# Attention scores as fp32 products of two tokens, values streamed against loaded probabilities, context divided on VectorE as it leaves PSUM

## Chip, cores and metric

One NeuronCore of one Trainium2 chip. The metric is the device time of one execution in microseconds (us); each kernel is given by the median of several runs.

## What is computed

A transformer block on x of shape (4, 512, 512), that is 2048 tokens of 512 features, in fp32. The attention is not over the sequence: each token has 32 heads of 16 features, and the 32 heads of a token attend to each other.

```python
q = (x @ wq.T + bq).reshape(B, S, 32, 16)      # k and v the same way
scores = einsum('bshd,bstd->bsht', q, k) / 4   # 32 x 32 for each token
context = einsum('bsht,bstd->bshd', softmax(scores), v).reshape(B, S, 512)
x = layernorm(x + context)
h = silu(x @ dq(w1).T) * (x @ dq(w2).T)        # 1376 hidden
x = layernorm(x + h @ dq(w3).T)
```

dq quantises blocks of 64 weights to the 16 NF4 levels and back, in the kernel. The layernorm has no gain and no offset.

## The kernel before

The order on each engine is written out by hand, with semaphores. There are three stages.

**Projection.** 48 turns tau: 4 blocks of 512 tokens, in each 4 turns for q, 4 for k, 4 for v. `project(tau)` makes 12 fp32r products of 512 columns into one of three PSUM banks. For q and k, three bf16 parts are split off: `part_high` (ScalarE, L810), `part_rest` (VectorE, L1186), `part_middle` (ScalarE, L819), `part_low` (VectorE, L1194); SyncE stores them to `qk_parts` in DRAM in runs of 272 bf16 (L588). ScalarE's `value` (L824) gives v, stored to `v_blocks`.

**NF4 levels.** 19 units of weights have 15 levels each, 285 in all. ScalarE's `steep` (L769) makes `nf_y`, VectorE's `lift` (L1154) takes it into `nf_acc`; three `nf_y` buffers stand between them. The tables LV_P, LV_A, LV_T and LV_F say how many levels are done in each turn of the projection, of the attention, at its end and in each step of the feed-forward: 59, 55, 5 and 166. GpSimd normalises a unit ahead of its levels and scales it after them.

**Attention.** 32 groups G of 64 tokens (16 token indices i in each of four quarters q). `load_stacks` (L423) brings, for every half block (4 groups), 12 pieces from `qk_parts` into `q_st` and `k_st`: 128 partitions hold the six products of bf16 parts, so one bf16 product of 128 rows gives the scores of one token. `scores(G)` (L1019) makes 64 products with 32 stationary and 32 streaming columns, four quarters in the four column groups of the array. VectorE: `highest`, `shift`, and a group later, after ScalarE's `exp`, `swap`, which transposes blocks of 32x32 to `probT`. `values(G)` (L1034) makes 16 fp32 products: stationary is `v_bd`, 128 rows (4 quarters of 32 heads) by 68 columns (4 times 16 features and a column of ones, for the sum), streaming is `probT` of 32 columns. ScalarE's `context` (L837) copies the 68x512 result to `ctx`. Once per block, `turn(("ct", b, k))` transposes heads back in five turns of 7, 7, 7, 7 and 4 heads, and VectorE's `add_context` (L1218) takes the reciprocal of the sums, multiplies and adds to the residual `part`. Then come the moments (VectorE), the norm (ScalarE) and `turn(("xt", ...))`, which transposes x1 for the feed-forward.

PE's order in a group is scores(G), ct turns, values(G - 2), xt turns. `v_bd_0` lies over memory that the projection uses, so GpSimd's `clear` (L716) and the load of it come after the last projection turns; the second `v_bd` after all parts and values are stored. `q_st`, `k_st` of the first half block are loaded from tau 37 on (FIRST_LOAD).

**Feed-forward.** 44 steps, each of 24 products for gate and up and 12 for down, with 512 columns, while the levels that are left go on. The last block's context turns and x1 turns lie in steps 2 to 7.

Of the kernel before, what the change touches and what calls it, by code (L numbers as in the profile page):

```python
# [14 lines left out]
P = 128  # L15
# [19 lines left out]
def layer_kernel(nc, x, wq, bq, wk, bk, wv, bv, w1, w2, w3, out):  # L35
# [18 lines left out]
    MV = Q4 * DV  # L54

    Q_TERMS = (0, 1, 2, 0, 1, 0)
    K_TERMS = (0, 0, 0, 1, 1, 2)  # L60

    TS = TB + 16
# [32 lines left out]

    def turns_of(u):

        kind, g, _ = UNITS[u]
        return [("f", u, s) for s in range(2 if kind == "w" else -(-len(GROUPS[g]) // 2))]
# [14 lines left out]
    def parts_of(u):  # L114
# [6 lines left out]
    NQK, NV, NPV = 5, 4, 4  # L121
# [5 lines left out]
    qk_d = nc.dram_tensor("qk_parts", [2, NHB, 3 * E, TS], BF16, kind="Internal").ap()  # L127
# [35 lines left out]
    HEADS = [range(0, 7), range(7, 14), range(14, 21), range(21, 28), range(28, 32)]  # L163
    CT_AT, XT_AT, MOMENTS_AT, NORM_AT, F_AT = {}, {}, {}, {}, {}
    for b in range(NBK - 1):
        for k in range(len(HEADS)):
            CT_AT.setdefault(8 * b + 10 + k // 2, []).append(("ct", b, k))
        MOMENTS_AT[8 * b + 12] = b
        NORM_AT[8 * b + 13] = b
        for c in range(KC):  # L170
            XT_AT.setdefault(8 * b + 14 + c // 2, []).append(("xt", b, c))

    LATE = {8 * b + 8 + k: 8 * b + 13 for b in range(NBK - 1) for k in range(2)}
    CONTEXT_AT = {}
# [59 lines left out]
    with ExitStack() as both, ExitStack() as proj, ExitStack() as att:  # L234
# [19 lines left out]
        crec = sb("crec", [P, 2, 7 * Q4], F32)  # L254
# [12 lines left out]
        room = sb("room", [P, 2 * H * (TS - TB) // 2 + MV * TI], F32, proj)  # L267
# [3 lines left out]
        qk_p = sb("qk_p", [P, NQK, 3, BK + TS - TB], BF16, proj)  # L271
        qk_r = sb("qk_r", [P, 3, BK], F32, proj)
# [40 lines left out]
        s_zero = sem("s_zero")  # L313
# [1050 lines left out]
```

## Time and profile before

| | |
|---|---|
| median of 3 runs | 787.52 us (786.13 to 788.67) |
| the profiled execution: its own time | 788.01 us |
| its span (first to last instruction) | 786.2 us |
| PE busy, share of the span | 732.7 us, 93% |
| VectorE (DVE) | 633.4 us, 81% |
| ScalarE (ACT) | 484.6 us, 62% |
| GpSimd (POOL) | 106.8 us, 14% |
| mean granted TensorE clock | 0.862 of full |
| DMA | 117.89 MB in 89474 packets |

In the span the projection ends at 165.6 us, the attention runs to 380 us, the feed-forward to the end. A busy PE is one with instructions in flight, not one at its peak. A time in the rows is counted from the span's start.

### The profile page before, as it was taken

Reading aid. Unit: us, or ns where it says so; the run is one execution under the profiler, and the core shown is the slowest. Engines: PE = TensorE matmul, PEld = TensorE weight load, DVE = VectorE, ACT = ScalarE, POOL = GpSimd, SP = SyncE. Lnnn points to the kernel's source line nnn. Section 1 sums busy time; section 2 is a strip of 40 time slices with the busy share of each in tenths; the row PEclk is TensorE's granted clock in tenths of the full one; section 3 lists DMA queues with packets and bytes.
Section 4 is the critical chain, followed back from the end, with each engine's and each line's share of the span. In section 5 each row is a group of like instructions: output and inputs, shape, how many; then the busy total and the mean of one; then the engine's idle time right before and its main releaser. Section 6 shows DMA issues by size and latency. Waiting matters only on the chain.

```text
span 786.2 us, 14305 instructions
## 1 busy us (share of the span) xinstructions
PE 732.7 (93%) x5688; PEld 625.5 (80%) x5688; DVE 633.4 (81%) x876; ACT 484.6 (62%) x650; POOL 106.8 (14%) x101
## 2 busy tenths in 40 slices
PE   4899999966999989999999999999999999999983
PEld 4778788856999989999888877887887788888761
DVE  2699999975888988988888899999977986554386
ACT  3588979773645636546853878877756775333134
POOL 2011012113101101111101121121201111000022
PEclk9999999995555655555799999999999999999995
DMA  9964455999797695995413371211514010330347
GB/s 219 223 182 146 134 166 167 250 305 271 166 261 189 184 283 134 269 216 202 163 26 122 120 230 54 81 39 31 173 59 155 1 61 21 134 119 13 121 147 160
DMA packets 89474, 117.89 MB, mean 150 GB/s; under 512 B 24768, under 2 KB 70848, under 8 KB 86496
## 3 DMA queue, kind: packets, MB, share of 16 engines
q1 hardware_dynamic: 88272, 114.88, 51.6%
q10 hardware_dynamic: 1136, 2.10, 1.2%
q8 instruction: 45, 0.74, 0.4%
q14 instruction: 21, 0.17, 0.1%
HBM read 76.42 MB, written 38.86 MB: 147 GB/s over the span
## 4 chain that ended last, share of the span: by engine, by line
PE 54%; DVE 18%; issue 11%; ACT 8%; DMA 4%; SPq 4%; POOL 1%; DVEq 0%; POOLq 0%; ACTq 0%
PE ps_p L1043 10%; DVE nf_acc L1166 8%; PE ps_s L947 7%; PE ps_s L945 7%; PE ps_s L946 7%; PE ps_p L945 5%; PE ps_p L947 5%; PE ps_p L946 5%; ACT nf_y L777 4%; PE ps_s L1030 3%; PE ps_t L968 2%; DMA qk_parts<-qk_p 2%; DVE part L1298 2%; DMA k_st<-qk_parts 1%; ACT part L852 1%
## 5 line engine op out<-in xcount | busy, mean ns | idle before, releaser
L1166 DVE SCALAR_TENSOR_TENSOR nf_acc<-nf_y,nf_acc 128x1024 f32<-128x1024 f32 (+4 forms) x266 | 298.5, 1122 | 37.6 <-ACT nf_y L777 28.3
L777 ACT ACTIVATE nf_y<-nf_w,bound_b 128x1024 f32<-128x1024 f32 (+4 forms) x285 | 288.9, 1047 | 9.7 <-DVE nf_acc L1162 3.4
L1043 PE MATMUL ps_p<-probT,v_bd 128*68 128x32 f32 x1024 | 125.7, 301 | 7.9 <-issue 7.9
L1043 PEld LDWEIGHTS ps_p<-probT,v_bd 128*68 128x68 f32 x1024 | 122.7, 211 | 9.4 <-issue 8.0
L945 PE MATMUL ps_p<-x_hl,w_hl 128*128 128x512 f32 x192 | 77.6, 404 | 6.1 <-DVE w_hl L1184 4.1
L695 POOL TENSOR_TENSOR nf_w<-nf_w,nf_rec 128x1024 f32<-128x1024 f32 (+4 forms) x19 | 39.5, 2080 | 320.1 <-DVE nf_rec L1150 320.1
L1325 DVE TENSOR_TENSOR silu<-silu,ps_s 128x512 f32<-128x512 f32 (+1 forms) x44 | 30.1, 684 | 61.5 <-PE ps_s L947 61.5
L927 ACT ACTIVATE hid_hl<-silu 128x512 fp32r<-128x512 f32 (+1 forms) x44 | 27.8, 632 | 77.6 <-DVE silu L1325 77.6
L947 PE MATMUL ps_p<-x_hl,w_hl 128*128 128x512 f32 x192 | 75.5, 393 | 0.0
L945 PE MATMUL ps_s<-x_hl,f_ha 128*128 128x512 f32 x192 | 75.4, 393 | 0.0
L946 PE MATMUL ps_p<-x_hl,w_hl 128*128 128x512 f32 x192 | 75.3, 392 | 0.0
L947 PE MATMUL ps_s<-x_hl,f_la 128*128 128x512 f32 x192 | 75.1, 391 | 0.0
L946 PE MATMUL ps_s<-x_hl,f_ha 128*128 128x512 f32 x192 | 75.0, 391 | 0.0
L834 ACT ACTIVATE prob<-prob 128x512 f32<-128x512 f32 x32 | 20.4, 638 | 86.4 <-DVE prob L1209 86.4
L922 ACT ACTIVATE silu<-ps_s 128x512 f32<-128x512 f32 (+1 forms) x44 | 26.2, 595 | 66.1 <-PE ps_s L947 66.0
L702 POOL TENSOR_TENSOR nf_acc<-nf_acc,nf_max 128x1024 f32<-128x1024 f32 (+4 forms) x19 | 37.6, 1977 | 209.7 <-DVE nf_acc L1166 209.6
L947 PE MATMUL ps_s<-x_hl,f_lb 128*128 128x512 f32 (+1 forms) x160 | 62.4, 390 | 0.0
L945 PE MATMUL ps_s<-x_hl,f_hb 128*128 128x512 f32 (+1 forms) x160 | 62.4, 390 | 0.0
L946 PE MATMUL ps_s<-x_hl,f_hb 128*128 128x512 f32 (+1 forms) x160 | 62.3, 390 | 0.0
L1030 PE MATMUL ps_s<-k_st,q_st 128*32 128x32 bf16 x2048 | 44.5, 249 | 9.0 <-issue 6.9
L1030 PEld LDWEIGHTS ps_s<-k_st,q_st 128*32 128x32 bf16 x2048 | 40.0, 171 | 13.5 <-issue 11.5
L945 PEld LDWEIGHTS ps_p<-x_hl,w_hl 128*128 128x128 f32 x192 | 36.5, 190 | 14.7 <-issue 5.4
(110 smaller groups left out, 1253.1 us busy)
## 6 DMA issues: line engine op xcount, KB each, us to landing
x_hl<-x_parts SPq DMA_DIRECT2D x10, 2048.0 KB, 8.5
qk_parts<-qk_p SPq DMA_DIRECT2D x64, 204.0 KB, 2.6
q_st<-qk_parts SPq DMA_DIRECT2D x48, 272.0 KB, 6.8
k_st<-qk_parts SPq DMA_DIRECT2D x48, 272.0 KB, 7.2
x_parts<-x_st SPq DMA_DIRECT2D x16, 512.0 KB, 4.4
nf_w<-in_L_ffn_w SPq DMA_DIRECT2D x24, 256.0 KB, 3.0
dequantised<-nf_acc SPq DMA_DIRECT2D x10, 512.0 KB, 2.6
v_blocks<-v_t SPq DMA_DIRECT2D x16, 256.0 KB, 3.5
```

The lines of the kernel that those rows point to most:

```text
L695: pool.tensor_tensor(v, v, nf_rec[0:p, 0:w // QBLOCK].unsqueeze(2).to_broadcast([p, w // QBLOCK, QBLOCK]), ALU.mult).then_inc(s_nnorm, 1)
L702: pool.tensor_tensor(acc, acc, nf_max[0:p, u % 2, 0:w // QBLOCK].unsqueeze(2).to_broadcast([p, w // QBLOCK, QBLOCK]), ALU.mult).then_inc(s ...
L777: act.activation(nf_y[0:p, at % NY, 0:w], nf_w[0:p, u % 2, 0:w], ACT.Identity, bias=bound_b[0:p, i:i + 1], scale=STEEP).then_inc(s_ny, 1)
L922: act.activation(silu[0:rows, s % 2], ps_s[0:rows, 0], ACT.Silu).then_inc(s_silu, 1)
L927: act.activation(hid_hl[0:rows, s % 2, 0], silu[0:rows, s % 2], ACT.Copy).then_inc(s_hh, 1)
L945: pe.matmul(dst, wh, rh, start=start, stop=False)
L946: pe.matmul(dst, wh, rl, start=False, stop=False)
L947: return pe.matmul(dst, wl, rh, start=False, stop=stop)
L1030: t = pe.matmul(ps_s[32 * q:32 * q + 32, G % 2, i * H:(i + 1) * H], q_st[:, :, s], k_st[:, :, s], start=True, stop=True)
L1043: t = pe.matmul(ps_p[0:MV, (G + 3) % NPV, i * H:(i + 1) * H], v_bd[hb % 2][:, :, g * GI + i], probT[:, G % 2, i], start=True, stop=True)
L1166: dve.scalar_tensor_tensor(out=acc, in0=y, scalar=float(NF4[i + 1]), in1=acc, op0=ALU.min, op1=ALU.max).then_inc(s_nacc, 1)
L1325: dve.tensor_tensor(h, h, ps_s[0:rows, 1], ALU.mult).then_inc(s_hid, 1)
```

## The change

- q and k stay fp32. ScalarE alone evacuates them (`queries_keys`, one operation), VectorE evacuates v (`value` moves from ScalarE). Each of the 32 q and k tiles is stored by one DMA of 128x16 runs of 36 fp32 (144 bytes; 32 tokens and 4 of padding) instead of two of 128x3 runs of 544 bytes.
- Scores: a product covers two tokens j. Stationary is `q_st`, 32 rows (2 tokens of 16 features) by 32 heads; streaming is `k_st`, 32 rows by 64 columns, zero where row and column are of different tokens. The four quarters sit on the diagonal of the array (rows 32q, columns 32q). 32 products per group instead of 64, fp32 instead of bf16.
- Values: `probT` (32 columns) is stationary and `v_bd` (68 columns, 68 fp32 apart) streams; four tokens go to the four column groups. VectorE's new `divide(G)` takes reciprocals of the 128x16 sums and multiplies 128x256 out of PSUM into `ctmp`. PE's new `back(G)` makes 4 transposes of `ctmp` (64 stationary, 128 streaming columns), and `context` copies 64x512.
- The context turns are four of eight heads, and `add_context` is one addition.
- Loads: queries one DMA per half block, keys eight of 16 partitions, zeros of `k_st` by GpSimd. The first keys, values and queries are loaded from tau 29, 31, 33, 37, 39 on, and `v_bd_0` is cleared at tau 12.
- Levels: LV_P 72, LV_A 45, LV_T 5, LV_F 163 of its 166.

```diff
-    TS = TB + 16
+    MC = Q4 * D
+    VS = TI + 4
+    J2, TN = 2, TI // 2
+    KS = TN + 4
...
+    FIRST_LOADS = {3 * KC * (NBK - 1) + at: what for at, what in ((-7, "keys 0"), (-5, "values 0"), (-3, "keys 1"),
+                                                                  (1, "queries 0"), (3, "queries 1"))}
-    LV_P = [1, 1, 1, 1, 1, 1, 1, 1, 2, 2, 2, 2] * NBK
+    LV_P = [0, 0, 0, 1, 2, 2, 2, 1, 2, 2, 2, 2] + [2, 2, 1, 2, 2, 1, 2, 2, 1, 2, 1, 2] * (NBK - 1)
     LV_P[-3:] = [1, 0, 0]
-    LV_A = [2] * GG
+    LV_A = [2, 1] * (GG // 2)
...
@@ sync
-                    for e in range(2):
-                        sp.dma_start(qk_d[i, 2 * b + e].rearrange("(a f) t -> f a t", a=3)[P * m:P * m + P],
-                                     qk_p[:, n % NQK, :, TB * e:TB * e + TS]).then_inc(s_stq[n % NQK], 16)
+                    sp.dma_start(qk_d[i, 2 * b:2 * b + 2, :, :, Q4 * m:Q4 * m + Q4].rearrange(
+                        "e q j r h n -> (r h) (e q j) n"), qk_p[:, n % NQK]).then_inc(s_stq[n % NQK], 16)
...
@@ scalar
+                act.activation(qk_p[:, n % NQK, :, 0:TN], ps_p[:, tau % 3].rearrange("p (a n) -> p a n", n=TN),
+                               ACT.Identity, bias=bias[:, i, m:m + 1]).then_inc(s_qh, 1)
...
@@ tensor
-                for i in range(GI):
+                for i in range(GI // J2):
                     for q in range(Q4):
-                        s = q * TI + g * GI + i
-                        t = pe.matmul(ps_s[32 * q:32 * q + 32, G % 2, i * H:(i + 1) * H],
-                                      q_st[:, :, s], k_st[:, :, s], start=True, stop=True)
+                        rows, n = slice(32 * q, 32 * q + 32), GI // J2 * g + i
+                        t = pe.matmul(ps_s[32 * q:32 * q + 32, G % 2, J2 * H * i:J2 * H * (i + 1)],
+                                      q_st[hb % 2][rows, :, n],
+                                      k_st[hb % 2][rows, :, :, n].rearrange("d j h -> d (j h)"), start=True, stop=True)
...
@@ tensor
-                wait(pe, s_ctx, G - NPV + 1)
+                wait(pe, s_evac, G - 1)
                 for i in range(GI):
-                    t = pe.matmul(ps_p[0:MV, (G + 3) % NPV, i * H:(i + 1) * H], v_bd[hb % 2][:, :, g * GI + i],
-                                  probT[:, G % 2, i], start=True, stop=True)
+                    a, j = divmod(i, 4)
+                    token = TN * (i % J2) + GI // J2 * g + i // J2
+                    t = pe.matmul(ps_p[32 * j:32 * j + 32, G % 2, a * MV:(a + 1) * MV], probT[:, G % 2, i],
+                                  v_bd[hb % 2][:, :, token], start=True, stop=True)
                 t.then_inc(s_pv, 1)
+            def back(G):
+                pe.wait_ge(s_evac, G + 1)
+                wait(pe, s_ctx, G - 1)
+                for a in range(4):
+                    t = pe.transpose(ps_p[0:MC, 2 + G % 2, P * a:P * a + P], ctmp[:, G % NCT, a * MC:(a + 1) * MC],
+                                     ident[:])
+                t.then_inc(s_back, 1)
...
@@ vector
+            def divide(G):
+                dve.wait_ge(s_pv, G + 1)
+                src = ps_p[:, G % 2, 0:4 * MV].rearrange("p (a q d) -> p a q d", q=Q4, d=DV)
+                rec = crec[:, G % 2].rearrange("p (a q) -> p a q", q=Q4)
+                dve.reciprocal(rec, src[:, :, :, D]).then_inc(s_crec, 1)
+                dve.wait_ge(s_crec, G + 1)
+                wait(dve, s_back, G - NCT + 1)
+                dve.tensor_tensor(ctmp[:, G % NCT].rearrange("p (a q d) -> p a q d", q=Q4, d=D), src[:, :, :, 0:D],
+                                  rec.unsqueeze(3).to_broadcast([P, 4, Q4, D]), ALU.mult).then_inc(s_evac, 1)
```

PE's order from the end of the projection into the attention, of the kernel before (the last number of a row is the count of the same instruction in a row; `ps_s` are scores, `ps_p` the values' result):

```order
601 L1030 MATMUL ps_s<-k_st,q_st 32x32 x192
602 L1043 MATMUL ps_p<-probT,v_bd 68x32 x16
603 L1030 MATMUL ps_s<-k_st,q_st 32x32 x64
604 L1043 MATMUL ps_p<-probT,v_bd 68x32 x16
605 L1030 MATMUL ps_s<-k_st,q_st 32x32 x64
```

The same place in the changed kernel:

```order
601 L1012 MATMUL ps_s<-k_st,q_st 32x64 x96
602 L1029 MATMUL ps_p<-v_bd,probT 32x68 x16
603 L1012 MATMUL ps_s<-k_st,q_st 32x64 x32
604 L1029 MATMUL ps_p<-v_bd,probT 32x68 x16
605 L1038 MATMUL ps_p<-ident,ctmp 64x128 x4
```

A group is 32 products of 64 columns and 16 of 68 instead of 64 of 32 and 16 of 32, and four transposes are added one group later.

VectorE's order in the attention before, two groups with context turns:

```order
197 L1205 TENSOR_REDUCE smax<-ps_s 128x16
198 L1215 STREAM_TRANSPOSE probT<-prob 128x512
199 L1209 TENSOR_TENSOR prob<-ps_s,smax 128x512
200 L1225 RECIPROCAL crec<-ps_t 128x28
201 L1228 TENSOR_TENSOR y_tmp<-ps_t,crec 128x448
202 L1232 TENSOR_TENSOR part<-part,y_tmp 128x7x4x16
203 L1225 RECIPROCAL crec<-ps_t 128x28
204 L1228 TENSOR_TENSOR y_tmp<-ps_t,crec 128x448
205 L1232 TENSOR_TENSOR part<-part,y_tmp 128x7x4x16
206 L1166 SCALAR_TENSOR_TENSOR nf_acc<-nf_y,nf_acc 128x1088
```

And a plain group and one with context turns in the changed kernel:

```order
154 L1200 TENSOR_REDUCE smax<-ps_s 128x16
155 L1210 STREAM_TRANSPOSE probT<-prob 128x512
156 L1204 TENSOR_TENSOR prob<-ps_s,smax 128x512
157 L1167 SCALAR_TENSOR_TENSOR nf_acc<-nf_y,nf_acc 128x1088 x2
158 L1218 RECIPROCAL crec<-ps_p 128x16
159 L1221 TENSOR_TENSOR ctmp<-ps_p,crec 128x256
160 L1200 TENSOR_REDUCE smax<-ps_s 128x16
161 L1210 STREAM_TRANSPOSE probT<-prob 128x512
162 L1204 TENSOR_TENSOR prob<-ps_s,smax 128x512
163 L1167 SCALAR_TENSOR_TENSOR nf_acc<-nf_y,nf_acc 128x1088
164 L1218 RECIPROCAL crec<-ps_p 128x16
165 L1221 TENSOR_TENSOR ctmp<-ps_p,crec 128x256
```

The reciprocal and the multiplication now stand in every group, behind its levels.

## Rows read from the trace of the kernel before

**Rows 1.** Windows by stage: length, busy us (instructions) per engine, granted clock, DMA share, GB/s

```profile
25.00:165.60 140.60, 135.43 (x618) 110.56 (x617) 131.02 (x153) 117.88 (x156) 19.94 (x15) 0.99 0.66 186
165.60:187.00 21.40, 8.05 (x229) 7.65 (x232) 11.81 (x14) 9.12 (x10) 6.33 (x9) 0.68 1.05 304
187.00:380.00 193.00, 186.61 (x3025) 180.85 (x3025) 162.32 (x244) 108.12 (x143) 19.85 (x10) 0.54 0.83 219
380.00:770.00 390.00, 383.98 (x1748) 311.62 (x1746) 309.73 (x422) 235.76 (x324) 49.73 (x33) 0.99 0.27 90
```

**Rows 2.** Timeline from projection to attention: start, length, engine, line, op, [idle <- releaser]

```profile
165.25 0.39 PE L947 MATMUL ps_p<-x_hl,w_hl 128*128 128x512 f32 x1
167.19 2.48 PE L1030 MATMUL ps_s<-k_st,q_st 128*32 128x32 bf16 x128 [1.56 <-DMA k_st<-qk_parts]
174.31 0.84 PE L1030 MATMUL ps_s<-k_st,q_st 128*32 128x32 bf16 x33 [3.49 <-issue]
179.65 3.84 POOL L726 MEMSET v_bd<- 128x1088 f32 x4 [19.23 <-DMA v_blocks<-v_t]
183.06 3.92 PE L1043 MATMUL ps_p<-probT,v_bd 128*68 128x32 f32 x32 [7.91 <-issue]
186.92 1.34 PE L1030 MATMUL ps_s<-k_st,q_st 128*32 128x32 bf16 x62
```

**Rows 3.** Timeline of PE in the attention

```profile
198.61 1.34 PE L1030 MATMUL ps_s<-k_st,q_st 128*32 128x32 bf16 x64
199.88 3.95 PE L1043 MATMUL ps_p<-probT,v_bd 128*68 128x32 f32 x32
203.77 1.35 PE L1030 MATMUL ps_s<-k_st,q_st 128*32 128x32 bf16 x64
...
234.26 1.85 PE L968 MATMUL ps_t<-ident,ctx 68*128 68x68 f32 x14
235.90 3.88 PE L1043 MATMUL ps_p<-probT,v_bd 128*68 128x32 f32 x32
```

**Rows 4.** Timeline of PE, transposes of x1 and what follows

```profile
255.47 1.95 PE L972 MATMUL ps_t<-ident,part 128*128 128x128 f32 x8
257.35 1.33 PE L1030 MATMUL ps_s<-k_st,q_st 128*32 128x32 bf16 x64
```

**Rows 5.** Windows, instructions of L1043 alone: PE, PEld, granted clock, DMA share, GB/s

```profile
265.60:269.00 3.40, 3.40 (x30) 3.40 (x30) 1.00 0.97 240
270.80:274.20 3.40, 3.40 (x30) 3.40 (x31) 0.50 1.03 246
```

**Rows 6.** Groups of VectorE from 187 to 380 us: count, busy us, mean ns, idle before

```profile
L1166 DVE SCALAR_TENSOR_TENSOR nf_acc<-nf_y,nf_acc 128x1088 f32<-128x1088 f32 (+1 forms) x48 | 61.6, 1282 | 20.3 <-ACT nf_y L777 19.8 <-DVE nf_acc L1166 0.5
L1209 DVE TENSOR_TENSOR prob<-ps_s,smax 128x512 f32<-128x512 f32 x29 | 18.9, 652 | 0.0
L1232 DVE TENSOR_TENSOR part<-part,y_tmp 128x448 f32<-128x448 f32 (+1 forms) x15 | 8.8, 585 | 0.5
L1228 DVE TENSOR_TENSOR y_tmp<-ps_t,crec 128x448 f32<-128x448 f32 (+1 forms) x15 | 8.8, 584 | 0.5
L1225 DVE RECIPROCAL crec<-ps_t 128x28 f32<-128x28 f32 (+1 forms) x15 | 4.6, 304 | 0.0
L1150 DVE RECIPROCAL nf_rec<-nf_den 128x17 f32<-128x17 f32 (+1 forms) x4 | 1.0, 255 | 0.0
```

**Rows 7.** Groups of the whole span that belong to the projection

```profile
L1197 DVE TENSOR_TENSOR qk_p<-qk_r,qk_p 128x512 bf16<-128x512 f32 x32 | 23.8, 745 | 0.0
L1190 DVE SCALAR_TENSOR_TENSOR qk_r<-ps_p,bias,qk_p 128x512 f32<-128x512 f32 x32 | 23.8, 742 | 4.0 <-ACT qk_p L816 3.8
```

**Rows 8.** Timeline of ScalarE, two turns of the projection

```profile
73.51 0.69 ACT L816 ACTIVATE qk_p<-ps_p,bias 128x512 bf16<-128x512 f32 x1 [0.47 <-PE ps_p L947]
76.23 0.69 ACT L816 ACTIVATE qk_p<-ps_p,bias 128x512 bf16<-128x512 f32 x1 [0.47 <-PE ps_p L947]
```

**Rows 9.** Windows with stores of 544-byte runs, stores of v, loads of 256-byte runs

```profile
71.50:73.00 1.50, 1.50 (x8) 1.27 (x7) 1.50 (x3) 1.50 (x2) 0.00 (x0) 1.00 0.93 276
61.00:62.00 1.00, 1.00 (x6) 0.60 (x4) 1.00 (x2) 1.00 (x2) 0.00 (x0) 1.00 0.77 262
334.20:335.80 1.60, 1.10 (x49) 0.93 (x42) 0.27 (x2) 0.00 (x0) 0.00 (x0) 0.50 1.32 166
```

More of the change, by code:

```diff
@@ L94, in layer_kernel, with pairs @@
     NU0 = len(GROUPS[0]) + 2
+    def pairs(g):
+        js, out = list(GROUPS[g]), []
+        while js:
+            n = 2 if len(js) > 1 and rows_of(js[1]) == P else 1
+            out.append(js[:n])
+            js = js[n:]
+        return out
     def turns_of(u):
         kind, g, _ = UNITS[u]
-        return [("f", u, s) for s in range(2 if kind == "w" else -(-len(GROUPS[g]) // 2))]
+        return [("f", u, s) for s in range(2 if kind == "w" else len(pairs(g)))]
     def valid(g):
@@ L396, in parts_stored @@
             for r in range(NQK):
-                wait(eng, s_stq[r], 32 * of_slot(tiles, r, NQK))
+                wait(eng, s_stq[r], 16 * of_slot(tiles, r, NQK))
         def values_stored(eng, tiles):
@@ L902, in _ @@
                     norm_1(NORM_AT[G])
-                steep(LV_A[G] - LV_A[G] // 2)
+            context(GG - 4)
+            for key in XT_AT.get(GG, []) + TAIL_1:
+                high(key)
             context(GG - 3)
-            for key in TAIL_1:
-                high(key)
-            context(GG - 2)
             steep(LV_T[0])
@@ L910, in _ @@
                 high(key)
-            context(GG - 1)
+            context(GG - 2)
             steep(LV_T[1])
@@ L1104, in _ @@
                 scores(G)
+                if G >= 2:
+                    values(G - 2)
                 for key in CT_AT.get(G, []):
                     turn(key)
-                if G >= 2:
-                    values(G - 2)
+                for at in BACK_AT.get(G, []):
+                    back(at)
                 for key in XT_AT.get(G, []):
@@ L1111, in _ @@
             values(GG - 2)
-            for key in TAIL_1:
+            for key in XT_AT.get(GG, []) + TAIL_1:
                 turn(key)
+            back(GG - 3)
             values(GG - 1)
@@ L1116, in _ @@
                 turn(key)
+            back(GG - 2)
             pe.wait_ge(s_minus_i, 1)
@@ L1120, in _ @@
                 gate_up(s)
+                if s == 0:
+                    back(GG - 1)
                 for key in F_TURNS.get(s, []):
@@ L1276, in _ @@
                     mean_shift(NORM_AT[G])
[L1277 removed]
+                lift(LV_A[G])
+                if G >= 2:
+                    divide(G - 2)
                 for key in CT_AT.get(G, []):
@@ L1283, in _ @@
                     low(key)
-                lift(LV_A[G] - LV_A[G] // 2)
             swap(GG - 1)
-            for key in TAIL_1:
+            divide(GG - 2)
+            for key in XT_AT.get(GG, []) + TAIL_1:
                 low(key)
@@ L1290, in _ @@
                 low(key)
+            divide(GG - 1)
             lift(LV_T[1])
```

267 lines of the change are left out of this document (110 added, 157 removed).

## The prediction

> **What bounds the kernel now.** I read the windows by stage first. In the projection PE is busy 135.4 of 140.6 us and VectorE 131.0; in the feed-forward PE 384.0 of 390 us [rows 1]. Neither leaves much to win. Between them lies the attention, from 165.6 to 380 us, 214.4 us, in two pieces. First a gap: the projection's last product starts at 165.25 and the first values start at 183.06; in the 21.4 us to 187 us PE is busy 8.05 us. The values wait for `v_bd`, which GpSimd could clear only at 179.65, after the stores of v [rows 2]. DMA is full there (share 1.05). From then on PE is busy 186.6 of 193 us [rows 1], and the timeline shows of what: a group takes from 198.61 to 203.77, 5.16 us, of which the 64 score products take 1.27 us and the 16 values products the other 3.89 us [rows 3]. VectorE is busy 162.3 of 193 us, so it stands close behind. The question is what PE's group becomes, and when VectorE takes over.
>
> **What PE's rate hangs on.** The order lists 16 values products, the trace 32 records: an fp32 product is two records, a bf16 product one. A values record takes 3.89 / 32 = 121 ns. This doesn't change with TensorE's clock: 30 records start in 3.4 us with 1.00 granted, and 30 with 0.50 [rows 5]. So it isn't array cycles. Its stationary operand is 68 columns that lie 256 bytes apart; 121 / 68 = 1.78 ns per column is my reading of a strided column. The scores' record, with both operands strided, takes 1.27 / 64 = 20 ns, in rounds of four that share the array, 80 ns a round.
>
> **Part by part, the projection.** Gone from VectorE are 32 x (745 + 742) ns = 47.6 us [rows 7]; added are 16 evacuations of v, about 0.68 us each as the nearest 128x512 operations, 11 us, and 13 levels of 1.28 us, 17 us. VectorE ends some 20 us lighter, ScalarE by the 32 middle parts and 16 values. PE's turn of 2.72 us (73.51 to 76.23) [rows 8] covers it all: a block of 20 levels asks of VectorE 20 x 1.28 + 8 x 0.68 + about 1.5 for the next unit, 32.5 us, against 12 x 2.72 = 32.6 us of products and four short transposing turns. Nothing is gained but part of PE's 5.2 idle us: **-1 us**. If that cover is gone it is VectorE's in-order evacuation of v that holds PE.
>
> The stores change: 128 x 16 runs of 144 bytes, 128 per DMA engine. In a stretch of 544-byte runs 276 GB/s moved, 31.5 ns per packet and engine; in one of 256-byte runs 166 GB/s, 24.7 ns [rows 9]. The line through both gives 22 ns at 144 bytes, 2.8 us a tile, 22.6 us for a block's eight. v takes 4 x 1 us at 262 GB/s [rows 9], NF4 loads and stores some 1.4 MB, 5 us. That is 31.7 of 33 us per block: it fits, barely, with five buffers to even it out. Cost 0, bounds 0 and the rival below.
>
> **The gap.** Keys, values and queries of the first half block are in place before the projection ends, and GpSimd clears at tau 12. What remains of 21.4 us is three groups at the new pace.
>
> **PE's group after.** *Scores*: 32 products, 64 records. The streaming operand is 64 columns 144 bytes apart: 64 x 1.78 = 114 ns a round of four, 28.5 ns a record, 1.8 us. Lower bound 64 x 20 ns = 1.28 us; upper bound 64 records one after the other. *Values*: 32 records, 68 columns streaming, again 121 ns, but four column groups side by side: 1.0 us; bounds 32 x 20 ns = 0.6 and, side by side in vain, 3.9 us. *Back*: 4 transposes with 128 streaming columns; eight such took 255.47 to 257.35, 0.235 each [rows 4]: 0.9 us. I take 3.8 us instead of 5.16, from the stride, since it explains both clocks. Over 32 groups 121 us; context turns 96 x 0.117 us (14 in 1.64 [rows 3]) = 11 us as before, x1 turns 48 x 0.235 = 11, the eight first weight turns 32 x 0.235 = 8. PE asks 151 us.
>
> **VectorE's attention after.** Busy now: 11.8 + 162.3 = 174.1 us [rows 1]. Ten levels fewer: -12.8 us. 15 context turns of 304 + 584 + 585 ns go: -22.1 us; 12 additions of 128x512 at some 0.68 us come: +8.2 us. `divide` in 32 groups: a reciprocal as 128x17, 255 ns, and 128x256 out of PSUM; 448 columns take 584 ns and 512 take 652 ns, so 256 some 380 ns [rows 6]: 0.635 x 32 = +20.3 us. Sum 167.7 us. **VectorE becomes the bound.** In the projection it reached 93%; here it waits for neighbours in a ring of scores, exp, swap, values and divide, so I take 94%: 178 us instead of 214.4, **-36 us**. A plain group is then near 4.6 us, with PE done in 3.8.
>
> New waits: PE's `back` waits for `divide`, behind it stand the xt turns and the next scores; `divide` stands a group earlier, so it costs nothing while VectorE isn't late. The ct turn waits for `context(G)`, one group later than before, behind levels on ScalarE (108 of 193 us busy, covered). SyncE's queue carries less: the score operands of a half block were 12 x 16 x 17.4 KB = 3.3 MB and are 2 x 128 x 4.6 KB = 1.2 MB.
>
> **Feed-forward.** 163 levels instead of 166, context additions 4 x 0.68 instead of 5 x 1.47 us, on VectorE, which PE covers (384 of 390): **-1 us**. Against that, 3 MB of weights and two x1 blocks must land in a shorter tail: 0 to +4 us, I take 0.
>
> Sum: -1 - 36 - 1 = -38 us against the profiled execution's 788.0: 750 us. The median of the runs is 0.5 us lower, so 749.5; I say 750.
>
> **Rivals.**
> *A, the streaming operand is read twice.* If each fp32 record fetches its strided columns in two passes, a round takes 228 ns in the scores and 242 in the values: 3.65 + 1.94 + 0.94 = 6.5 us a group. Then PE bounds: 32 x 6.5 + 30 = 239 us, +25, less 2: **811 us**. It turns slower from a group of 5.8 us on (32 x 5.8 + 30 = 216). For it: fp32 costs two records already. Against: nothing in the trace shows a strided streaming operand of fp32. Half way, at 5.5 us a group, the time is 779. The Trainium skill (SBUF — State Buffer, the note on 16-byte cachelines) says that fp32 strided by more than four elements pays at each new line; by that rule all three strided operands pay, as I assumed, and the trace's 1.78 ns per column agrees.
> *B, the four quarters don't run side by side*, since their row groups write one PSUM bank. A record alone costs at least the 117 ns of a 68-column transpose [rows 3]: 64 x 0.117 = 7.5 us a group, 9.4 in all, 302 + 30 = 332 us: **900 us**. Slower from 80 ns a record on. The old scores also wrote one bank from four column groups, but from the same rows. The Trainium skill (TensorEngine Tiling (Array Packing), PSUM Pressure) says that different row tiles cannot access the same bank simultaneously; that speaks against this change, and no row here decides it.
> *C, the 144-byte stores choke the projection.* At 22 ns a packet there is 1 us per block to spare; at 44 ns a tile takes 5.6 us and a block 45 + 9 = 54 us against 33, four times +21: **834 us**. ScalarE would wait for its buffer, PE for PSUM. It turns slower than before when a packet costs over some 32 ns. For it: the rows for 256 bytes are hardly cheaper than for 544. The Trainium skill (DMA: Bandwidth & Descriptors, Specifications) puts line rate at 512 bytes and more, with a read-modify-write below; the rows only show reads below that size, so this stays a rival.
> *D, VectorE packs better*, at 98%: 171 us, **743 us**, or ScalarE's relief helps the feed-forward too: 735.
>
> **How the numbers follow.** Main case 0.60 (739 to 762), A 0.17 (765 to 811), B 0.05, C 0.10 (765 to 834), D 0.08. Range 735 to 800: it leaves out B, most of C and A's worst end, about 0.18. A measurement of this kernel tells 0.3%, 2.4 us, from no change. Faster is main, D and the milder half of A and C: 0.81; same 0.02; slower 0.17.
>
> **What would show it.** Right: first values a few us after the projection, a plain group at 4.2 to 4.9 us, VectorE over 92% busy in the attention, score records near 28 ns, values near 30 ns. Wrong: PE over 95% busy there with a group above 5 us (A); score records above 80 ns (B); ScalarE's evacuation waiting for its stores, turns of more than 2.8 us (C).

## The result, and the profile after

The changed kernel takes **768.03 us** (median of 4 runs, 766.25 to 770.44) against 787.63 us of the kernel before (786.13 to 788.67, four runs on the same chip): ratio 0.9755, 95% interval 0.9723 to 0.9786. It is 19.6 us faster, half of the 38 us predicted. The time lies inside the range (735 to 800), and above the main case's own range (739 to 762); it is inside by the width that was left for rivals A and C. The profiled execution took 770.44 us, its span is 768.6 us.

The windows by stage of the changed kernel (columns as in [rows 1]):

```profile
20.00:166.00 146.00, 132.04 (x600) 107.34 (x598) 111.72 (x113) 99.33 (x116) 29.92 (x19) 0.95 1.18 148
166.00:179.00 13.00, 10.38 (x36) 7.67 (x36) 10.06 (x10) 9.19 (x10) 4.74 (x3) 0.87 1.28 119
179.07:356.90 177.83, 143.32 (x3373) 117.75 (x3372) 163.38 (x276) 101.25 (x139) 18.68 (x16) 0.85 0.61 151
356.90:361.00 4.10, 0.10 (x2) 0.10 (x1) 4.07 (x8) 4.10 (x8) 0.00 (x0) 0.85 0.98 416
361.00:768.60 407.60, 390.08 (x1758) 315.55 (x1758) 300.31 (x435) 237.24 (x327) 53.78 (x39) 0.97 0.29 95
```

And the timeline of its PE, with its waits in the projection, its first scores and values, and the first feed-forward product:

```profile
54.41 0.76 PE L929 MATMUL ps_p<-x_hl,w_hl 128*128 128x512 f32 x1 [11.47 <-DVE w_hl L1185]
...
166.37 0.50 PE L929 MATMUL ps_p<-x_hl,w_hl 128*128 128x512 f32 x1 [2.86 <-ACT qk_p L822]
...
171.65 0.50 PE L929 MATMUL ps_p<-x_hl,w_hl 128*128 128x512 f32 x1 [2.25 <-ACT qk_p L822]
...
179.07 5.05 PE L1012 MATMUL ps_s<-k_st,q_st 32*32 32x64 f32 x159
187.07 1.20 PE L1029 MATMUL ps_p<-v_bd,probT 128*32 128x68 f32 x32
...
360.93 0.77 PE L929 MATMUL ps_s<-x_hl,f_ha 128*128 128x512 f32 x1 [4.00 <-DMA x_hl<-x_parts]
```

The profiled executions of both kernels, stage by stage; the differences add up to that of the spans:

| stage | before | after | difference | predicted |
|---|---|---|---|---|
| to the first score product (before: to the projection's end) | 165.6 | 179.07 | **+13.5** | -1 |
| attention | 214.35 | 177.83 | **-36.5** | -36 |
| wait for x1 at the first feed-forward product | none | 4.03 | **+4.0** | 0 (bounds 0 to +4) |
| feed-forward | 406.25 | 407.67 | +1.4 | -1 |
| span | 786.2 | 768.6 | -17.6 | -38 |

The gap of 21.4 us in which PE was busy 8.05 us [rows 1] is gone: the values start 8 us after the scores. The granted clock, 0.54 in [rows 1], is 0.85 in the attention (in e9 below it is 0.79, and the attention isn't longer). What went wrong is the stage that I had priced at nothing. PE stands still three times in the projection, 11.47, 2.86 and 2.25 us, where the projection before had 5.2 idle us in all. The waits of ScalarE from 20 to 179 us (line, releaser: us in total, times, longest):

```profile
ACT qk_p L822 <- DMA queries_keys<-qk_p: 20.0, 5, 8.0
ACT qk_p L822 <- PE ps_p L931: 19.0, 13, 2.7
```

ScalarE waits 20 us for stores that free the five buffers `qk_p`. Its queue is in order, so a blocked evacuation also holds back the halves of the next unit's weights; VectorE waits for these, and PE for VectorE. That is why PE's largest wait names `w_hl` of VectorE. SyncE's DMA queue (17 to 62 us) shows the start of it: four loads of `part`, the last of 3.5 MB of x, stand ahead of the first store:

```profile
17.74 3.62 SPq L444 DMA_DIRECT2D part<-in_L_attn_hidden_states  x4
21.48 38.39 SPq L594 DMA_DIRECT2D queries_keys<-qk_p  x8
```

From 42 to 50 us, in which SyncE issues nothing but such stores, 77 GB/s move:

```profile
42.00:50.00 8.00, 0.94 (x7) 0.57 (x5) 3.07 (x4) 5.02 (x7) 0.00 (x0) 0.73 1.53 77
```

144 bytes x 16 engines / 77 GB/s = 29.9 ns for a packet, where my line through 544 and 256 bytes [rows 9] gave 22. That line also joined a store (544 bytes) to a load (256 bytes).

In the attention, the groups of VectorE that answer to [rows 6]:

```profile
L1167 DVE SCALAR_TENSOR_TENSOR nf_acc<-nf_y,nf_acc 128x1088 f32<-128x1088 f32 (+1 forms) x45 | 56.7, 1260 | 4.8 <-ACT nf_y L783 3.5
...
L1221 DVE TENSOR_TENSOR ctmp<-ps_p,crec 128x256 f32<-128x256 f32 x31 | 13.2, 425 | 1.1
L1185 DVE TENSOR_TENSOR x_st<-ps_t,x_st 128x512 fp32r<-128x512 f32 x12 | 8.0, 685 | 7.4 <-ACT x_st L809 7.4
L1230 DVE TENSOR_TENSOR part<-part,ps_t 128x512 f32<-128x512 f32 x12 | 7.6, 679 | 0.0
L1218 DVE RECIPROCAL crec<-ps_p 128x16 f32<-128x16 f32 x31 | 7.6, 245 | 0.0
```

Reciprocal and product cost 245 + 425 = 670 ns, priced at 635; an addition 679 ns, priced at 680. The one large wait left to VectorE is 7.4 us for ScalarE's part of `x_st` in the xt turns, and ScalarE there waits for a store:

```profile
ACT x_st L809 <- DMA x_parts<-x_st: 8.4, 5, 3.6
```

PE's records at either level of its clock, two groups (timeline, and windows that show the granted clock):

```profile
266.72 2.07 PE L1012 MATMUL ps_s<-k_st,q_st 32*32 32x64 f32 x64
268.72 1.19 PE L1029 MATMUL ps_p<-v_bd,probT 128*32 128x68 f32 x32
...
280.48 2.07 PE L1012 MATMUL ps_s<-k_st,q_st 32*32 32x64 f32 x64
282.48 1.18 PE L1029 MATMUL ps_p<-v_bd,probT 128*32 128x68 f32 x32
```

```profile
266.10:269.50 3.40, 3.40 (x96) 2.80 (x98) 3.37 (x8) 2.01 (x3) 0.00 (x0) 0.50 0.60 109
279.80:283.20 3.40, 3.40 (x96) 2.94 (x97) 3.37 (x7) 2.46 (x4) 0.00 (x0) 1.00 0.03 7
```

64 score records start in 2.00 us at 0.50 granted and in 2.00 us at 1.00: 31.3 ns each, a round of four 125 ns, 1.95 ns a column (predicted 28.5 ns and 1.78). A values record takes 35 ns (1.12 us from 268.72 to the start of the next transposes at 269.84, / 32), predicted 30.

### The profile page after: what moved, and what is told of

Its sections match the earlier page's. It is cut to its first block, busy times and chain, and to the rows that moved or that the text cites. A ratio compares the mean times of both kernels' runs of the same rounds, so it can differ in the third digit from the quotient of the medians.

```text
span 768.6 us, 14470 instructions
## 1 busy us (share of the span) xinstructions
PE 685.8 (89%) x5818; PEld 556.9 (72%) x5818; DVE 594.9 (77%) x846; ACT 458.1 (60%) x604; POOL 108.7 (14%) x99
## 4 chain that ended last, share of the span: by engine, by line
PE 58%; DVE 18%; DMA 10%; issue 8%; ACT 3%; SPq 1%; POOL 1%; DVEq 0%; POOLq 0%; ACTq 0%
PE ps_p L929 9%; PE ps_s L929 9%; PE ps_p L930 9%; PE ps_p L931 9%; PE ps_s L931 9%; PE ps_s L930 9%; DVE nf_acc L1167 7%; DMA queries_keys<-qk_p 4%; DMA x_parts<-x_st 2%; PE ps_s L1012 2%; DVE prob L1204 2%; DVE smax L1200 2%; DMA wst<-in_L_attn_wk 1%; DMA x_hl<-x_parts 1%; ACT part L845 1%
## 5 line engine op out<-in xcount | busy, mean ns | idle before, releaser
L1167 DVE SCALAR_TENSOR_TENSOR nf_acc<-nf_y,nf_acc 128x1024 f32<-128x1024 f32 (+4 forms) x266 | 313.7, 1179 | 43.2 <-ACT nf_y L783 31.8
L929 PE MATMUL ps_p<-x_hl,w_hl 128*128 128x512 f32 x192 | 78.9, 411 | 17.4 <-DVE w_hl L1185 11.5
L703 POOL TENSOR_TENSOR nf_w<-nf_w,nf_rec 128x1024 f32<-128x1024 f32 (+4 forms) x19 | 44.4, 2339 | 328.2 <-DVE nf_rec L1151 328.2
L930 PE MATMUL ps_p<-x_hl,w_hl 128*128 128x512 f32 x192 | 76.9, 401 | 0.0
L931 PE MATMUL ps_p<-x_hl,w_hl 128*128 128x512 f32 x192 | 76.9, 400 | 0.0
L911 ACT ACTIVATE hid_hl<-silu 128x512 fp32r<-128x512 f32 (+1 forms) x44 | 27.8, 632 | 75.7 <-DVE silu L1321 75.7
L1012 PE MATMUL ps_s<-k_st,q_st 32*32 32x64 f32 x2048 | 67.2, 291 | 5.0 <-issue 5.0
L1012 PEld LDWEIGHTS ps_s<-k_st,q_st 32*32 32x32 f32 x2048 | 58.1, 136 | 13.3 <-issue 13.0
L1029 PE MATMUL ps_p<-v_bd,probT 128*32 128x68 f32 x1024 | 38.1, 302 | 10.5 <-issue 5.4
L929 PEld LDWEIGHTS ps_s<-x_hl,f_ha 128*128 128x128 f32 x192 | 36.8, 191 | 12.3 <-issue 4.7
## 6 DMA issues: line engine op xcount, KB each, us to landing
queries_keys<-qk_p SPq DMA_DIRECT2D x32, 288.0 KB, 11.1
```

The costliest lines, as they stand in the source:

```text
L703: pool.tensor_tensor(v, v, nf_rec[0:p, 0:w // QBLOCK].unsqueeze(2).to_broadcast([p, w // QBLOCK, QBLOCK]), ALU.mult).then_inc(s_nnorm, 1)
L911: act.activation(hid_hl[0:rows, s % 2, 0], silu[0:rows, s % 2], ACT.Copy).then_inc(s_hh, 1)
L929: pe.matmul(dst, wh, rh, start=start, stop=False)
L930: pe.matmul(dst, wh, rl, start=False, stop=False)
L931: return pe.matmul(dst, wl, rh, start=False, stop=stop)
L1012: t = pe.matmul(ps_s[32 * q:32 * q + 32, G % 2, J2 * H * i:J2 * H * (i + 1)], q_st[hb % 2][rows, :, n], k_st[hb % 2][rows, :, :, n].rearra ...
```

## The experiments

They ran in three sets, each on one chip with the kernel before on it: e1, e2, e3 and e5 (before 787.05 us), then e4, e6, e7 and e8 (before 785.75), then e9 to e12 (before 787.96). The windows and waits are those of one profiled execution of each kernel. The second set has the unaltered changed kernel in it (e6). The first has not, but e2 has its projection and e1 its attention; in the third e9 has its projection. Three theories of the lost 20 us stood against each other: the order of SyncE's queue at the start, the price of 144-byte packets as such, and waits of PE or VectorE inside the attention.

### e1_x_late: the loads of x behind the first stores

```diff
-            for b in range(2, NBK):
-                for e in range(2):
-                    load_x(sp, b, e)
...
+                if tau in (10, 22):
+                    for e in range(2):
+                        load_x(sp, {10: 2, 22: 3}[tau], e)
```

> The changed kernel with the loads of x for blocks 2 and 3 (2 MB) issued at tau 10 and 22 instead of ahead of every store of q and k. Theory Q (the first stores queue behind 3.5 MB of x): PE's wait of 11.5 us in block 0 falls to under 3 us, the projection ends near 169 us instead of 179, the time is 758 to 760 us. Rival P (the packets of 144 bytes alone fill the DMA): 8 tiles at 3.7 us are 30 us of DMA in 22 us of products, and the wait stays at 8 us or more, time above 764 us.

Measured: 755.54 us (753.11 to 756.18), ratio 0.959 [0.9565, 0.9615]. The projection ends at 166.78. Waits of PE to 170 us, and of ScalarE for the stores:

```profile
PE ps_p L929 <- DVE w_hl L1185: 2.1, 1, 2.1
```

```profile
ACT qk_p L822 <- DMA queries_keys<-qk_p: 7.1, 3, 4.3
```

The wait of 11.5 us has become 2.1, with two of 1.5 and 1.4 us at the end of the projection. But this can't be set against the changed kernel's own profile, as the next run shows.

### e2_x1_first: the first load of x1 ahead of stores

```diff
-                for key in XT_AT.get(G, []):
-                    store_x1(key)
                 if G == GG - 1:
                     load_x1(0)
+                for key in XT_AT.get(G, []):
+                    store_x1(key)
```

> The changed kernel with the first x1 block's load issued ahead of the last two stores of x1 parts, as before the change. If those stores and their waits hold the load back, it is issued some 6 us earlier, PE's wait of 4.0 us at the first feed-forward product is gone and the time falls by 4 us to 764 us. If the wait is DMA bandwidth, it stays.

Measured: 757.81 us (756.76 to 759.88), ratio 0.9631 [0.9609, 0.9653]. In the changed kernel the loads of `x_hl` are issued behind four stores; here one goes between them:

```profile
344.35 6.39 SPq L552 DMA_DIRECT2D x_parts<-x_st  x4
350.85 1.70 SPq L565 DMA_DIRECT2D x_hl<-x_parts  x2
```

```profile
335.96 1.18 SPq L552 DMA_DIRECT2D x_parts<-x_st  x2
337.26 0.79 SPq L565 DMA_DIRECT2D x_hl<-x_parts  x1
340.76 2.46 SPq L552 DMA_DIRECT2D x_parts<-x_st  x2
```

PE's first feed-forward product then waits 1.6 us instead of 4.0, and for VectorE's `f_la`, no longer for the load. The edit is worth some 2 us (e1, of the same set and without it, waits 3.7). The rest of the gain isn't its own: with the changed kernel's projection code the projection ended at 170.93 here, not at 179.07, with a wait of PE in block 0 of 8.5 us. So in this set e1's edit is worth 170.93 - 166.78 = 4.1 us of projection, not 12, and the wait that it shortened was one of 8.5 us.

### e3_levels: the levels of NF4 as in the kernel before

```diff
-    LV_P = [0, 0, 0, 1, 2, 2, 2, 1, 2, 2, 2, 2] + [2, 2, 1, 2, 2, 1, 2, 2, 1, 2, 1, 2] * (NBK - 1)
+    LV_P = [1, 1, 1, 1, 1, 1, 1, 1, 2, 2, 2, 2] * NBK
...
-    LV_A = [2, 1] * (GG // 2)
+    LV_A = [2] * GG
```

13 levels fewer in the projection, ten more in the attention.

> The changed kernel with the level tables of before: 59 levels in the projection, 55 in the attention. Theory V (VectorE bounds the attention): ten levels of 1.28 us more lengthen it from 178 to 190 us, the projection stays within 2 us of 158 us, time 778 to 781 us. Rival (PE or the ring of waits bounds it): the levels fill VectorE's 13 idle us, attention under 182 us, time under 773 us.

Measured: 764.14 us (764.01 to 764.66), ratio 0.971 [0.9694, 0.9725]. The attention:

```profile
168.31:350.50 182.19, 142.37 (x3373) 118.81 (x3372) 174.56 (x286) 111.80 (x148) 19.17 (x11) 0.84 0.58 152
```

VectorE is busy 11.2 us more and the attention is 4.4 us longer than the changed kernel's (3 to 5 us longer than in e2 and e1 of the same set, 179.1 and 177.1 us). By the numbers written down this is the rival's outcome, not theory V's 190 us. But the added levels first fill the time in which VectorE stood for `x_st`, 7.4 us in the changed kernel and 8.8 in e2:

```profile
DVE x_st L1185 <- ACT x_st L809: 1.5, 2, 1.1
```

Against e8 below, which has no such wait (it ran in another set, and attentions that no edit touched measure 176 to 181 us), the same levels cost 182.19 - 170.46 = 11.7 us, near 10 x 1.26. So the stage is VectorE's, and what the expectation had left out were its waits.

### e5_twice: every q and k tile stored twice

Each of the 32 stores has a second one, of the same runs, to a tensor that nobody reads; a buffer is free when both have landed.

```diff
-                    sp.dma_start(qk_d[i, 2 * b:2 * b + 2, ...
+                    for home in (qk_d, qk_again):
+                        sp.dma_start(home[i, 2 * b:2 * b + 2, ...
```

> The changed kernel with every tile of q and k stored a second time, to a tensor that nothing reads (work added, output the same). It measures the packet of 144 bytes. At 29 ns a packet and engine a tile takes 3.7 us, a block 16 x 3.7 + 9 = 68 us instead of 34, the time grows by some 130 us to 900. At the 22 ns of the prediction a block takes 54 us, the time grows by 80 us to 850. At 15 ns it takes 40 us, and 25 us are added.

Measured, one run: 845.16 us; the projection ends at 250.25. Its windows and ScalarE's wait:

```profile
20.00:250.25 230.25, 163.83 (x642) 127.59 (x640) 119.94 (x124) 109.50 (x125) 33.90 (x22) 0.84 1.21 136
```

```profile
ACT qk_p L824 <- DMA again<-qk_p: 87.4, 18, 11.5
```

Against e2 of the same set 32 tiles cost 250.25 - 170.93 = 79 us, 2.5 us or 19 ns a packet and engine. That is a lower bound, since some of it went into slack, and it came out near what I wrote for 22 ns and far from what I wrote for 29. From above, the 228 us from the first store (22.29) to the projection's end, over all 64 tiles, give 27.8 ns, or an estimated 23 if the 9.1 us per block for v and NF4 are taken off. So this run leaves the mean price open between 19 and 28 ns and doesn't show that it was above the 22 of the prediction. The packets are a bound that lies just beside the projection's length, and the changed kernel's loss falls where they queue up.

### e6_again: the changed kernel once more

Nothing is altered; a control for this set.

> The changed kernel itself, unaltered, beside the others on one chip. The run with the x1 load moved gained 10 us, 8 of them before the place of its edit (its projection ended at 170.9 us against 179.1). If the waits for the first stores differ from chip to chip or run to run, this control comes at 760 to 768 us and not at 768 again; if they are fixed, it repeats 768 us within 2.

Measured: 766.85 us (763.51 to 767.52), ratio 0.9752 [0.9721, 0.9784]; the projection ends at 177.26, some 6 us later than with the same code in e2. The kernel before, meanwhile, differs by 0.3% at most between the sets. Where does it come from? One stretch of the stores in both, e2 and then e6:

```profile
43.00:49.00 6.00, 1.55 (x9) 1.06 (x7) 3.47 (x4) 5.42 (x7) 0.00 (x0) 0.87 1.54 91
```

```profile
43.00:49.00 6.00, 1.43 (x9) 0.96 (x7) 3.35 (x4) 5.21 (x7) 0.00 (x0) 0.85 1.63 80
```

91 GB/s in one set, 80 in the other: 25.3 and 28.8 ns a packet. e3 (first set) has 91 too; e8 and e4 (second set) 82 and 77; e9 (third set) 84; the profile of the changed kernel 80. The 144-byte stores run at a rate that goes with the set. Each set had its own chip and its own time, so whether it is the chip isn't shown. The projection's end follows the rate only roughly: e8, with this projection's code in this set, ended it at 174.64, 2.6 us before e6. So only kernels of one set may be compared in this stage, and between two single profiles a difference of under some 3 us says little.

### e4_first_late: the operands of the attention's first groups loaded later

The five loads of `FIRST_LOADS` go from tau -7 to +3 to tau 8 to 12, behind the last stores.

> The changed kernel with the first keys, queries and values loaded only at tau 44 to 48, at the end of the projection. If early loading is what closed the gap ahead of the attention, it comes back: keys, queries and values of two half blocks are 2.9 MB, some 12 us, and the time rises by 8 to 12 us against the control. If the gap had been closed by the cleared buffers alone, it rises by under 3 us.

Measured: 772.0 us (770.92 to 772.74), ratio 0.9825 [0.9795, 0.9855], 5.2 us slower than e6, between the two outcomes expected. ScalarE's waits for stores fall from 17.4 to 9.3 us and the last product of the projection starts at 170.99, and then:

```profile
170.99 0.39 PE L931 MATMUL ps_p<-x_hl,w_hl 128*128 128x512 f32 x1
183.82 2.42 PE L1012 MATMUL ps_s<-k_st,q_st 32*32 32x64 f32 x76 [12.44 <-DMA q_st<-queries_keys]
```

Against e6 the early loads take some 6 us from the projection (3 against e8), where they share the DMA engines with its stores, and save 12 behind it. The part of the change that closed the gap pays for itself.

### e7_both: e1 and e2 together

> Both edits of the order of DMAs: x of blocks 2 and 3 later, the first x1 load ahead of the stores. If their gains are at different places they add up: 755.5 less the 3.7 us wait, 751 to 753 us.

Measured: 760.14 us (759.68 to 760.45), ratio 0.9675 [0.9652, 0.9698]. The wait at the first feed-forward product is 1.5 us, as in e2, and the projection ends 3.6 us ahead of e6 (173.66 against 177.26), as in e1 against e2 (4.1), but only 1.0 us ahead of e8. What I expected missed because I had taken e1's 166.8 for a property of the code: of its distance to 179.1, some 4 us were the edit's and 8 went with the set. Against its control the two edits gain 6.7 us.

### e8_xt_spread: one xt turn per group

Two xt turns of a block stood in one group (in blocks 0 and 1 they now have one each), and each needs one of two `x1_st` buffers, which a store of 512 KB frees.

```diff
-            XT_AT.setdefault(8 * b + 14 + c // 2, []).append(("xt", b, c))
+            XT_AT.setdefault(8 * b + 14 + (c if b < 2 else c // 2), []).append(("xt", b, c))
```

> The changed kernel with the four x1 turns of blocks 0 and 1 in four groups instead of two. VectorE waits 7.4 us in the attention for ScalarE's x1 parts, which wait for the store of one of two buffers. If VectorE bounds the attention, these waits shrink to 3 us and the time falls by 3 to 5 us; if the ring does, nothing moves by over 1 us.

Measured: 758.62 us (757.91 to 759.14), ratio 0.9655 [0.9632, 0.9679], 8.2 us less than e6. The attention, and VectorE's wait for `x_st` in it:

```profile
174.64:345.10 170.46, 142.72 (x3373) 117.21 (x3372) 162.90 (x276) 100.72 (x139) 18.66 (x16) 0.86 0.62 155
```

```profile
DVE x_st L1185 <- ACT x_st L809: 0.4, 1, 0.4
```

VectorE's work is the same (162.90 us busy; e6 has 163.28), the attention is 7.0 us shorter than e6's 177.44, and VectorE is at 96% of it. The 7.4 us of waiting were 7 us of the kernel. The remaining 1.2 us are not the edit's: the projection ended 2.6 us earlier, with unaltered code, and the wait at the first feed-forward product is 1.4 us longer (4.9).

### e9_contig: both streaming operands without a stride

```diff
-                                      q_st[hb % 2][rows, :, n],
-                                      k_st[hb % 2][rows, :, :, n].rearrange("d j h -> d (j h)"), start=True, stop=True)
+                                      q_st[hb % 2][rows].rearrange("d h n -> d (h n)")[:, 32 * n:32 * n + 32],
+                                      k_st[hb % 2][rows].rearrange("d j h n -> d (j h n)")[:, 64 * n:64 * n + 64],
+                                      start=True, stop=True)
...
-                                  v_bd[hb % 2][:, :, token], start=True, stop=True)
+                                  probT[:, G % 2].rearrange("p i h -> p (i h)")[:, 4 * i:4 * i + MV],
+                                  start=True, stop=True)
```

> The changed kernel with contiguous operands in the scores (queries, keys) and a contiguous streaming operand in the values (probabilities in place of v); the output then isn't attention, the work is of the same shape. If the stride sets the pace (1.78 ns a column, the same at both clocks), the 64 score records fall from 2.0 us to 1.3 us and the 32 values records from 1.1 us to 0.65 us, at full clock. If the fp32 passes through the array set it, both stay as they are.

Measured, one run: 768.89 us, as the changed kernel. The attention, and two score turns, at the clock's two levels:

```profile
178.59:354.90 176.31, 115.13 (x3373) 92.46 (x3372) 162.87 (x275) 100.82 (x138) 18.65 (x16) 0.79 0.60 151
202.03:203.06 1.03, 1.03 (x65) 0.94 (x65) 1.03 (x2) 0.00 (x0) 0.00 (x0) 1.00 1.04 194
212.03:213.90 1.87, 1.87 (x66) 1.70 (x65) 1.87 (x3) 1.03 (x2) 0.00 (x0) 0.50 0.43 116
```

PE is busy 28 us less (115.13 against 143.32) and the attention is 1.5 us shorter. PE does not bound it. And without the stride the 64 score records take 1.03 us at 1.00 granted and 1.87 at 0.50, so they nearly follow the clock (the faster figure is below the 1.3 us expected); with it, 2.00 at both. In the scores the stationary operand lost its stride too. In the values only the streaming one did, and their 32 records take 0.68 us instead of 1.18, both at 1.00 granted:

```profile
203.06 0.68 PE L1030 MATMUL ps_p<-probT 128*32 128x68 f32 x32
```

### e12_q_runs: queries stored in runs of 1152 bytes

The q half of the tiles goes to a tensor of its own whose runs are q, j and n together, so 16 of the 32 stores have an eighth of the packets; the loads of the queries become eight each, with the small runs on their side.

```diff
+                    if i == 0:
+                        sp.dma_start(q_d[2 * b:2 * b + 2, Q4 * m:Q4 * m + Q4].rearrange("e r h q j n -> (r h) e (q j n)"),
...
-            eng.dma_start(q_st[hb % 2].rearrange("p h n -> p (h n)"),
-                          qk_d[0, hb].rearrange("q j d h n -> (q j d) (h n)")).then_inc(s_ldq[hb % 2], 16)
+            for a in range(Q4 * J2):
+                q, j = divmod(a, J2)
+                eng.dma_start(q_st[hb % 2][D * a:D * a + D], q_d[hb, :, :, q, j]).then_inc(s_ldq[hb % 2], 16)
```

> The changed kernel with the q tiles stored in another layout, 128 x 2 runs of 1152 bytes instead of 128 x 16 of 144; the loads of queries then take the runs of 144 bytes, in the attention, where DMA is at 0.61. It halves the small packets of the projection. If the packets are what holds the projection beyond the queue of x, ScalarE's waits for stores fall from 17 us to under 5 and the projection ends at 165 to 168 us; with the attention as long as before the time is 755 to 758 us. If the loads of 144 bytes choke the attention, PE waits for q_st there and the time is above 766 us.

Measured: 756.72 us (755.14 to 758.18), ratio 0.9607 [0.957, 0.9643]. The projection ends at 167.0; e9 of the same set, with the changed kernel's projection, ended it at 178.6. So most of the loss goes with the layout of these stores; the order of the queue is a part of it. The edit makes the runs fewer, longer and differently placed in DRAM at once; which of these counts wasn't tried apart. The attention, with the small loads in it, is 178.0 us, 1.7 longer than e9's. The store of a q tile lands 3.5 us after its issue, the median of the small-run tiles falls from 11.1 to 8.3:

```profile
x_parts<-x_st SPq DMA_DIRECT2D x16, 512.0 KB, 3.8
queries<-qk_p SPq DMA_DIRECT2D x16, 288.0 KB, 3.5
queries_keys<-qk_p SPq DMA_DIRECT2D x16, 288.0 KB, 8.3
```

### e10_all and e11_all_q_runs: the edits together

e10 is e1, e2 and e8, with four levels moved from the attention (`LV_A` 1 at groups 0, 2, 4 and 6) into block 0 of the projection (`LV_P` begins 1, 1, 1, 2, 2, ...), where VectorE had room. e11 is e10 with e12's queries.

> The changed kernel with later x loads, the first x1 load ahead of the stores, x1 turns spread over four groups, and four levels moved from the attention to the first turns of the projection. Projection to end at 167 to 173 us (as with later x loads alone), attention 170.5 - 4 x 1.28 = 165.5 us if VectorE bounds it, no wait above 2 us at the first feed-forward product: 744 to 751 us.

> Both of the above together. Projection to end at 164 to 166 us, attention 166 us, feed-forward 405: 738 to 745 us, about 4 to 6 us under the run without the new q layout. If the attention's small loads cost it, no better than that run.

Measured: e10 **750.29 us** (749.77 to 751.98), ratio to the kernel before 0.9535 [0.9505, 0.9565]; e11 750.59 (748.07 to 751.33), ratio 0.953 [0.9497, 0.9562]. The attention of e10, then of e11:

```profile
173.90:343.30 169.40, 142.10 (x3373) 117.61 (x3372) 159.90 (x271) 97.13 (x135) 19.27 (x17) 0.87 0.65 164
```

```profile
168.10:342.40 174.30, 144.61 (x3373) 118.94 (x3372) 159.06 (x271) 97.08 (x135) 18.24 (x16) 0.83 0.73 158
```

e10 lies in its range; its attention missed the 165.5 us expected. Four levels fewer took 5.2 us from VectorE's `lift`, but one operation of another kind, at the end of the projection, took 4.09 us where its like take 0.7, while GpSimd scaled a unit and cleared `v_bd` (172.16 to 178.81 us; whether one held up the other wasn't tried), and VectorE's waits are 2 us longer than in e8:

```profile
172.66 4.09 DVE L1165 TENSOR_SCALAR nf_acc<-nf_y 128x1088 f32<-128x1088 f32 x1
```

e11 missed its range of 738 to 745 us. Its projection ends 5.8 us earlier and its attention is 4.9 us longer: VectorE waits 6.1 us for `x_st` again, with the loads of small runs now inside the stage (DMA share 0.73 instead of 0.65). That they delay the stores of x1 is my reading and wasn't tried apart. In e12, against e9, the small runs moved from the stores to the loads gained 12 us; here, against e10, they gained nothing. e10's projection still ended at 173.9, 8 us behind the kernel before.

## Why the prediction was right in sign and half in size

- **"PE's turn covers it all ... -1 us" (the projection): wrong, +13.5.** The failed step is "That is 31.7 of 33 us per block: it fits, barely, with five buffers to even it out. Cost 0". Two things in it were off. The 22 ns a packet came from a line through a store of 544 and a load of 256 bytes and went on below the last point; where little else flows, the stores show 25 to 30 ns, by the set. Then the sum was a mean over a block, and what decides are its two ends: the stores of block 0 wait behind 3.5 MB of x (e1: worth 4.1 us in its set), and those of the last block share the engines with the early loads of the attention's operands (e4: 3 to 6 us). Five buffers, five tiles of about 3.5 us, do not even that out. How the 13.5 us divide between price and order stays open: e12 takes away 11.6 us and leaves the order as it is, and e5 doesn't exclude a mean price of 22 ns.
- **Rival C (144-byte stores) had the mechanism right**, down to "ScalarE would wait for its buffer, PE for PSUM" (20.0 us of waits, 4.9 in e12 with fewer packets), and the price at which it turns, 32 ns, was not reached. I had put it at 0.10 and its cost at 0 or +85; a rival that takes effect in part should have been in the sum. With a packet at 25 to 30 ns a block's eight tiles take 25.6 to 30.7 us of DMA, with the 9.1 us for v and NF4 35 to 40 us against 33, and four blocks miss by 7 to 27 us; the measured 13.5 lies there. That is no proof of the price, since such a sum slows every block alike, and the trace has its waits in block 0 (11.47 us) and in the last (2.86 and 2.25), with PE busy for all of 82 to 95 us. Taking the 24.7 ns of 256 bytes [rows 9] as the floor of the price would have said 34.4 us a block and +6 at least.
- **"The gap": right.** Values come 8 us after the first scores.
- **The scores, values and back turns: right.** Predicted 1.8, 1.0 and 0.9 us, measured 2.00, 1.12 and between 0.56 (from 198.49 to 199.05) and 1.00 (from 265.72 to 266.72, at 0.50 granted). That makes 3.7 to 4.1 us against 3.8. A (a second reading) would have shown 57 ns a score record, B (no side by side) 117; 31 was measured. The 117 is a poor measure for B, since it is that of another operation; e9 gives a better one: its score records start every 16 ns (1.03 us / 64), and the products of the projection, 12 of 512 columns in 2.72 us [rows 8], take 0.44 ns a column, 28 ns for 64 columns, so more than one record was under way. This decides against the sentence of the Trainium skill (TensorEngine Tiling (Array Packing), PSUM Pressure) as I had read it: four row groups write one bank here, each in columns of its own, and run side by side. B's turning point was also off: by A's own limit of 5.8 us a group it is some 61 ns a record, not 80.
- **"VectorE becomes the bound ... -36 us": right, 36.5**, with two small errors that cancel. It is busy 163.4 us, 4.3 less than summed, and at 92%, not 94%. e9 (PE 28 us lighter, 1.5 us gained) and e8 against e3 (10 levels, 11.7 us) show the bound from both sides. What kept it from 96% was not the ring of neighbours that I named but the two `x1_st` buffers.
- **The first feed-forward product: inside the bounds "0 to +4", at their bad end.** I took 0 without looking at what stands ahead of the load of x1 in SyncE's queue; stores of x1 do, and e2 shows that passing two of them is worth about 2 us.
- **"Feed-forward: -1": +1.4**, below what its spread over these kernels (404.9 to 408.4 us) can tell.

## What to carry to other kernels

When a store's layout is changed, count the packets per DMA engine and price them at no less than the smallest run already seen, then ask what the queue holds at the start and not on average: a stage at 95% of its DMA has no room for a queue. When the bound passes from PE to VectorE, the next microseconds lie in what VectorE waits for in order (here a buffer that a store must free for ScalarE); spreading the turns that need it over more groups gained 7 us of attention with no work removed. Where a transfer stands at its edge, take a control in every set: the same code ended its stage 6 to 8 us apart in two sets and 2.6 us apart within one, and the kernel without such transfers showed nothing of it.

## What the runs showed of the hardware

- Score products with both fp32 operands in strides of 144 bytes take 1.95 ns a streaming column (a round of 64 in 125 ns) at both levels of TensorE's clock; without the strides a round takes 64 ns at 1.00 granted and 117 at 0.50 (1.03 and 1.87 us / 16 rounds). The values, where only the streaming stride (272 bytes) was taken away, go from 1.18 to 0.68 us for 32 records of 68 columns. The Trainium skill (SBUF — State Buffer, the note on 16-byte cachelines) says that a large stride pays at each new line; the trace agrees, and adds that this price isn't the clock's.
- Four products on the array's diagonal (rows 32q, columns 32q), writing four parts of one PSUM bank, run side by side: 31 ns a record, 16 ns without the stride (e9), less than the 28 ns that 64 columns take at the projection's pace (0.44 ns a column at 1.00 granted).
- Stores in runs of 144 bytes move 77 to 91 GB/s where SyncE issues nothing else, 25 to 30 ns a packet and engine, and the figure goes with the set, each on another chip: 91 GB/s in e2 and e3, 77 to 82 in e4, e6 and e8, 84 in e9, from 43 to 49 us of each. Why wasn't tried.
